# Value matmuls ahead of the output projection matmuls in each key tile of a fused attention and expert-projection kernel

## The reference, cut to what matters

```python
q = moe_proj(q_proj); k = moe_proj(k_proj); v = moe_proj(v_proj)   # 4096 x 128 each
# moe_proj(p): y = einsum('nc,ech->neh', x, p); einsum('ne,neh->nh', w, y)
scores = einsum('bth,bsh->bts', q, k) / sqrt(h)
attn = softmax(scores, axis=-1)
o = einsum('bts,bsh->bth', attn, v).reshape(n, h)
z = einsum('ne,nh->enh', w, o)
out = einsum('enh,ehc->nc', z, o_proj)      # 16 experts, 128 -> 256 each
...
return x + gb * out
```

## Time and profile before

| | us |
|---|---|
| median of three runs | 1512.7 |
| the profiled execution | 1513.24 |
| its span, first to last instruction | 1511.5 |
| attention part, from block 1's first scores to the end | 573 |
| of one query block in its middle (blocks 2, 3) | 78 |

### The profile page before, as it was taken

One profiled execution on the slowest core, in us unless ns is written; L12 is line 12 of the kernel. 1 busy time (PEld: TensorE's weight loads), 2 busy tenths in 40 slices (PEclk: granted clock), 3 DMA queues, 4 the chain that ended last, 5 costly groups with the idle time before them and its releaser, 6 DMA issues. The chain is left out here.

```text
span 1511.5 us, 23593 instructions
## 1 busy us (share of the span) xinstructions
PE 1404.2 (93%) x6880; PEld 1206.6 (80%) x6880; DVE 1181.6 (78%) x2173; ACT 686.1 (45%) x1344; POOL 718.2 (48%) x598
## 2 busy tenths in 40 slices
PE   5669999999999999999999776999999999999997
PEld 3458999999999899999999554877777777777875
DVE  6767676775867758675767797999999999999765
ACT  3240301203022030220110666887888788888974
POOL 2230121312113121130100586898888788888997
PEclk8689999999999999999999898999999999999998
DMA  4230000000000000000030020000000000000000
GB/s 133 70 92 19 26 27 24 27 16 20 27 25 28 17 20 27 25 13 16 25 119 5 9 70 0 15 22 15 16 22 16 22 14 21 14 12 11 21 16 21
DMA packets 62794, 42.90 MB, mean 28 GB/s; under 512 B 13728, under 2 KB 59728, under 8 KB 62672
## 3 DMA queue, kind: packets, MB, share of 16 engines
q1 hardware_dynamic: 48432, 33.85, 7.4%
q10 hardware_dynamic: 14240, 7.61, 1.7%
HBM read 26.49 MB, written 14.94 MB: 27 GB/s over the span
## 5 line engine op out<-in xcount | busy, mean ns | idle before, releaser
L1318 PE MATMUL ps<-w_hi,memory_r 128*128 128x384 f32 x2048 | 567.4, 343 | 5.8 <-DVE w_lo L768 2.6
L1118 DVE SCALAR_TENSOR_TENSOR wst<-ps,w_cur,wst 128x384 f32<-128x384 f32 x480 | 295.5, 616 | 195.6 <-PE ps L1318 189.9
L1557 POOL TENSOR_TENSOR memory<-memory,pf 128x512 f32<-128x512 f32 x248 | 363.9, 1467 | 71.7 <-ACT pf L1681 60.8
L1318 PEld LDWEIGHTS ps<-w_hi,memory_r 128*128 128x128 f32 x2048 | 376.0, 189 | 15.7 <-DVE wst L1115 6.8
L1318 PE MATMUL ps<-w_lo,memory_r 128*128 128x384 f32 x1024 | 344.5, 336 | 0.0
L1766 DVE TENSOR_TENSOR p_lo<-pf,p_hi 128x512 fp32r<-128x512 f32 x256 | 296.9, 1162 | 30.6 <-ACT p_hi L1683 29.4
L1318 PEld LDWEIGHTS ps<-w_lo,memory_r 128*128 128x128 f32 x1024 | 193.9, 189 | 3.0
L1681 ACT ACTIVATE pf<-ps 128x512 f32<-128x512 f32 x256 | 153.0, 598 | 93.6 <-PE ps L1881 74.6
L1746 DVE TENSOR_REDUCE mx<-ps 128x1 f32<-128x512 f32 x224 | 149.3, 678 | 13.5 <-PE ps L1870 13.5
L1627 ACT COPY ps<-shift_rows 128x512 f32<-128x512 f32 x256 | 152.7, 597 | 6.2
L1683 ACT ACTIVATE p_hi<-ps 128x512 fp32r<-128x512 f32 x256 | 152.2, 594 | 0.0
(11 more groups left out here) (212 smaller groups left out, 2144.2 us busy)
## 6 DMA issues: line engine op xcount, KB each, us to landing
memory<-in_x SPq DMA_DIRECT2D x8, 512.0 KB, 4.2
x_scratch<-memory SPq DMA_DIRECT2D x8, 512.0 KB, 3.0
x2b<-x_scratch SPq DMA_DIRECT2D x32, 128.0 KB, 2.1
out_x<-memory SPq DMA_DIRECT2D x32, 128.0 KB, 1.7
qk_scratch<-wst ACTq DMA_DIRECT2D x28, 128.0 KB, 2.2
memory<-qk_scratch SPq DMA_DIRECT2D x9, 256.0 KB, 5.0
memory<-in_o_proj SPq DMA_DIRECT2D x1, 2048.0 KB, 9.1
v_scratch<-wst ACTq DMA_DIRECT2D x28, 64.0 KB, 1.9
```

The source lines that it names most:

```text
L1118: nc.vector.scalar_tensor_tensor(out=dst, in0=src, scalar=w, in1=dst, op0=ALU.mult, op1=ALU.add).then_inc(moe_acc, 1)
L1318: ins = nc.tensor.matmul(ps[:, s % MOE_BANKS, 0:H3], x_part[p][:, k, rows], w_part[:, k, e].rearrange("p t h -> p (t h)"), start=(k == 0 a ...
L1557: nc.gpsimd.tensor_tensor(p_sum[:, p], p_sum[:, p], pf[:, j % PB], ALU.add).then_inc(p_summed, 1)
```

## The change

Two calls in TensorE's `body` change places: `values` is issued ahead of `project` in every step from 2 to 33 of query blocks 1 to 7. No other engine's instructions move, and no wait is added or removed; each keeps its wait with it.

```diff
                         if not first and j == 1:
                             sums(*before(i, p))
+                        if j >= LAG:
+                            values(i, p, j - LAG)
                         if not first and j >= LAG:
                             project(*before(i, p), j - LAG)
-                        if j >= LAG:
-                            values(i, p, j - LAG)
                         if not last and j == NT - 2:
                             broadcast_shift(*following(i, p))
```

## The result

The changed kernel takes 1523.84 us in the median of four runs (1522.27 to 1525.89), the one before 1512.89 beside it (1511.63 to 1514.2): a ratio of 1.0075, with a 95% interval of 1.0061 to 1.009. It is slower by 11 us, and the forecast was 1521 with 1512 to 1528 around it. The profiled spans are 1511.5 and 1521.3, so 9.8 us of it can be followed in the traces.

A forecast was written before the change was run, and what follows sets the result against it. Blocks 1 to 6 were taken as bound by TensorE with small stops, block 7 by GpSimd. Seams of 7.60 + 1.22 + 0.78, less 1.0 for step 4, made 8.6 us slower: 1521, range 1512 to 1528.

The forecast's parts named there:

- Term 1: Middle of a block: values wanting p_lo 0.68 us earlier and later projections are covered by spare time, cost 0.
- New waits in steps 5 to 27: Sign against the forecast: new TensorE waits in these steps would mean the middle is not covered.
- the rival of the uncovered middle: Delayed VectorE work in the middle adds half the bound, 6.0 us, giving 1527 (1533 with all); chance 0.14.
- the other side: Later accumulations let GpSimd through first, stops in the middle and step 4 go: -3.6 us, 1509; chance 0.10.
- Term 2: Each block's end, tile 28: TensorE waits 1.0 us for p_lo, and all that follows is 0.68 us late.
- Term 3: Block's end, tile 31: late piece 29 puts GpSimd's sum ahead of p_lo; 1.22 us late in all, then 0.68 for order.
- Term 4, 3|4: Seam at the loop's end: ScalarE's pause hides TensorE's last 0.68 us, so 1.22 us comes through.
- Term 5: Clock after long waits, at the loop's turn and block 7's end: 0, with bounds -3.8 and +9.6 us.
- Term 4, 6|7: Seam into block 7: GpSimd is 1.12 us late by itself, so 0.78 of 1.90 us comes through.
- Block 7 unchanged in length: Sign for the forecast: the length of block 7 stays as it was.
- Term 4, the stop in step 4: Blocks 2, 3, 5 and 6: the stop in step 4 mostly stays; 0.25 us back in each, 1.0 in all.
- The rival of the covered seams: GpSimd and VectorE catch up at the seams, step 4's stop goes whole: +0.6 to +2.8 us, 1514.5; chance 0.18.

The follow-up runs named there:

- experiment 1: Kernel before, with values ahead of project only in steps 2 to 29, steps 30 to 33 in the old order; 1513.2 against 1512.51 us, ratio 1.0003.
- experiment 5: Changed kernel, with VectorE's accumulation of piece 29 moved behind p_lo of tile 31; 1525.21 us against 1513.45 for the kernel before.
- experiment 7: Changed kernel, VectorE's accumulation of piece 29 behind p_lo of tile 31 and ScalarE's scaling of piece 28 one step later; 1518.65 us, 1.0039 of the kernel before.
- Experiment 4: Kernel before, with values ahead of project only in step 30 (tile 28); 1513.54 against 1512.51 us, one execution.
- experiment 3: Kernel before, with values ahead of project only in step 33, the last tile; 1514.89 against 1512.51 us, one execution.
- experiment 6: Changed kernel, but step 33 in the old order; 1519.22 us against 1513.45 for the kernel before, ratio 1.0043.
- experiment 2: Kernel before, with values ahead of project only in steps 30 to 33; 1520.2 against 1512.51 us, ratio 1.0049.
- experiment 9: Kernel before, with VectorE's max piece reductions ahead of p_lo in steps 3 to 26; 1504.07 against 1513.16 us, ratio 0.9946.

## Why the prediction was right, and where it was not

**Term 1, the middle at 0: right in sum, partly by luck.** Up to step 30 blocks 3 and 5 became 0.2 us shorter, and experiment 1 shows 1.0003. The blocks are less alike than I took them. Block 2 loses 1.3 us, because its stop in step 4 went; block 1 gains 1.5, from new stops in step 4 (0.88), step 15 (0.78) and at tile 26 in step 28 (0.84). Block 6 has the same two new stops in steps 15 and 28. New waits in steps 5 to 27 stood among the signs that I am wrong, and in these two blocks the middle is indeed not covered; the gain in block 2 makes up for it, which I had not foretold. As a whole the rival of the uncovered middle failed, and so did the other side: the stops for max pieces hold 16.7 us where they held 16.4.

**Term 2, tile 28: right in blocks 2 to 5,** 0.94 to 0.99 us of waiting for 1.0 foretold. In blocks 1 and 6 tile 26 waits instead, two steps earlier, for 0.84.

**Term 3, tile 31: the size right, the cause half.** The wait before the values is 1.44 to 1.48 in blocks 2 to 5 (1.33 in 1 and 6) where 1.4 was foretold, and the seam of block 3 is +1.93 for +1.90. The margin of 0.19 us on which the pair's change of owner hung turned out as 1172.68 - 1172.22 = 0.46, on the foretold side. The step that failed is "Its accumulation [...] can start only then", taken as the whole reason. ScalarE's scaling of piece 28 makes p_hi late by as much, so experiment 5 gained nothing, and with both moved the wait went (experiment 7). The working also had the owner change only when piece 29 is late twice, for tile 28 and for its own place. Experiment 4 has the first delay alone, and the sum is ahead of p_lo already, so the seam's 1.9 is the plain sum of experiments 3 and 4. The last p_lo takes 1.37 us, a little under the 1.5 that I named as a sign. I had said of ScalarE that it "has about 1 us to spare before its seed is wanted"; that was about the seeds, and I had not followed its queue to p_hi of the last tile.

**Term 4, 3|4: mis-sized, by 2.6 us.** "TensorE's last 0.68 is hidden: 1.22" gave block 4 its forecast, and it became +3.88. The hidden part was there: from scores(0) to scores(2) it was 5.07 us and is 4.21. But only ScalarE's pause was counted. VectorE's, already in the trace of before as a row of idle time, starts when its last accumulation ends, and the change puts that behind the last matmul of the block:

```profile
1173.06 0.69 DVE L1746 TENSOR_REDUCE mx<-ps 128x1 f32<-128x512 f32 x1 [2.51 <-PE ps L1870]
```

That is before, where VectorE's last accumulation of block 3 had ended at 1170.54; the matmul that the row names had started at 1170.94 and doesn't explain 2.51 us. After has 2.56 at 1179.46, above. What follows on TensorE after:

```profile
1179.81 0.50 PE L1879 MATMUL ps<-memory_r 128*128 128x512 f32 x1 [1.45 <-ACT ps L1627]
...
1182.33 0.80 PE L1894 MATMUL ps<-p_hi,v_hi 128*128 128x512 f32 x1 [1.30 <-DVE p_lo L1766]
```

The working, up to scores(4), in us: 0.86 gained at the seed, 1.47 lost before the values of tile 0, and 1.2 lost by the clock, together +1.9 (with rounding) where -0.68 was foretold; the end of the block adds its 1.94, foretold as 1.90. Experiments 3 and 6 show it from both sides: the order of step 33 alone makes block 4 longer by 3.77, and to take it back gives 2.44. The pause accounts for the 1.47; the 1.2 of the clock is another matter (term 5).

**Term 4, 6|7: right in kind.** Block 7 starts 12.04 us later on TensorE and its first copy on GpSimd 11.38 later, so GpSimd's own lag was used up in part, 0.66 and not 1.12. (The sign "Block 7 unchanged in length" did not fit this term, by which it is 1.12 shorter on TensorE.)

```profile
1418.85 0.73 POOL L1528 TENSOR_TENSOR memory<-memory 128x256 f32<-128x256 f32 x1 [1.43 <-DVE memory L1783]
1419.51 0.61 POOL L1553 COPY memory<-pf 128x512 f32<-128x512 f32 x1
```

GpSimd ended the output tile of the block before only when VectorE's last accumulation was done, which now stands behind the last projection. Up to the sums block 7 became 0.84 us shorter (72.55 for 73.39); the stretch behind them is taken up with the clock, below.

**Term 4, the stop in step 4: 0.25 a block was a poor mean.** It went whole in block 2 (1.15 to 0.13), stayed in blocks 3 and 5 (1.16 and 1.15 to 1.25 and 1.24), came down from 1.07 to 0.88 in block 6, and block 1 got one of 0.88 that it had not had. The rival of the covered seams had this part right for other kernels: in experiments 2, 3 and 4, where only the end is changed, the stop is gone in all four blocks. Why the changed middle brings it back in blocks 3 and 5 and not in block 2 stays open.

**Term 5, the clock at 0: small in sum, by luck.** The new waits of 0.95 and 1.48 at the seams lowered nothing, since the mean over block 3 is 1.00. At the turn it cost more than before. The stretch behind the wait for p_lo (length, busy time, granted clock, DMA):

```profile
1182.30:1187.90 5.60, 5.57 (x13) 0.51 0.14 47
```

These are 13 matmuls at 0.43 us from start to start, at the lower of the two levels, 1.2 GHz, where it was 8. (The prediction read 0.40 off busy time; the starts are 0.43 apart there too.) It is tempting to put the difference down to two waits of 1.44 and 1.47 us close together in place of one of 2.31, but the other traces don't bear that out: experiment 7 has two waits of 1.61 and 1.49 at the same place and 9 matmuls at the lower level, and experiment 9 has one of 2.36, as before, and 14. So the 1.2 us can't be counted as the change's, nor can a part of what experiments 6 and 7 gain in block 4. At the very end the sums row takes 1.05 us for 1.87, at the upper level at first, and the stretch behind it is 1.36 shorter. I had put a gain there down to a shorter wait, and the wait is shorter, 2.20 for 2.89. But experiment 1, with a wait of 2.88, shows the sums at 1.06 us, and experiment 3, with one of 2.20, shows them at 1.87. So the length of the wait doesn't settle it, and how much of that 1.36 belongs to the change stays open.

**Sum.** Forecast 8.6, measured 9.8 in the spans. Block 4 missed by +2.66, block 1 by +0.63, block 7 by -1.09, block 2 by -0.98, block 6 by -0.54, the others by 0.1; 0.39 lies ahead of the attention. The time is good partly because misses cancel: 1.2 us that the clock took in block 4 stand against 1.36 at the end of block 7, and neither was foretold. The medians differ by 11, and the 1.2 us between that and the spans is within what single runs scatter.

## What to carry to other kernels

An instruction that is put ahead of another spends the spare time of what it waits for, and that spare time can be spent once; work it out for each step, the last ones of a block above all, and for each engine that feeds it, not for the first feeder found. Before an operation is moved to the end of a loop's pass, look up for each engine when its last instruction of the pass can end, because the pause at the turn starts there. And where an instruction that never queues for the shared port stands behind one that does, try it ahead: of all that was tried here, that alone made the kernel faster, and it did so by spending the same spare time.

## What was not expected of the hardware

- At the turn of the loop VectorE stands for 2.51 to 2.56 us as ScalarE does for 2.46, and TensorE only waits for them. That pause is as long as eleven matmuls, and it starts only when the engine's own last instruction ends.
- The port pair is handed over whole, in both directions. Of the 224 p_lo of blocks 1 to 7 before, 149 take over 0.75 us, and every one of them ends 0.54 or 0.55 us after the end of a GpSimd instruction; alone it takes 0.67. Of GpSimd's 217 sums there, 112 take over 1.35 us; each of these started while a p_lo ran and ended 1.14 to 1.17 after it, for 1.26 alone. So the one that waited needs about 0.1 us less, from the other's end on, than it takes alone.
- The length of the stretch at the lower clock level behind the turn varied with no cause that these traces show: 8 to 10 matmuls in some kernels, 13 or 14 in others, with one long wait or with two shorter ones.
- VectorE's busy share says little of what is wanted of it. Its busy time in block 3 was 75.4 us before, 73.3 after (1.8 us longer) and 70.8 in experiment 9 (2.4 us shorter), since its instructions count the time in which they are blocked.
